# The residual of a fused Mamba and LoRA layer added by TensorE transposes in the output's PSUM bank, not by VectorE

## The reference

```python
x = x + _L0_attn_ref(_L0_cond_ref(x, itok_B_0_15, W, lora_A, lora_B), A_log, D, x_proj_w, dt_proj_w, dt_proj_b)
x = x + _L0_ffn_ref(_L0_cond2_ref(x, itok_B_6_15, base_weight, base_bias, lora_A_w, lora_B_w), router_w, A, B)

# cond:  x @ W + (x @ A[id]) @ B[id]              one adapter per batch
# attn:  dt = softplus(dt_in @ dt_proj_w.T + b)   h_t = exp(dt A) h_(t-1) + dt B_t u_t
#        y_t = sum over 16 states of h_t C_t + D u_t
# cond2: x @ W2.T + bias + LoRA of the batch
# ffn:   gates = softmax over the top 2 of 4 experts, delta = sum over experts of gate * 4 * (mid @ B.T)
```

## Time and profile before

| | |
|---|---|
| median of 3 runs | 912.07 us |
| lowest, highest | 908.38, 920.36 us |
| span of the profiled execution | 918.8 us, mean granted TensorE clock 0.958 |
| PE, DVE, ACT, POOL busy | 90%, 83%, 70%, 72% of the span |
| chain that ended last | PE 64%, DVE 9%, POOL 7%, DMA 6%, ACT 6%, issue 5% |
| from `out` 0's addition in one group to the next group's, groups 1 to 6 | 104.6, 104.2, 107.1, 109.2, 104.0 us |

### The profile page before, as it was taken

How to read it: one execution, slowest core, us unless ns; L and a number is a source line. 1 busy time by engine, 2 the same in 40 slices (tenths; PEclk the granted TensorE clock), 3 DMA queues, 4 the chain that set the end, 5 groups by cost and what they waited for, 6 DMA issues and landing times.

```text
span 918.8 us, 18601 instructions
## 1 busy us (share of the span) xinstructions
PE 830.7 (90%) x6416; PEld 769.3 (84%) x6416; DVE 764.1 (83%) x688; ACT 638.7 (70%) x1481; POOL 661.9 (72%) x344
## 2 busy tenths in 40 slices
PE   5898999899999999799997998999998999888885
PEld 4888998799888988799877997789987998677772
DVE  2437788898999799988997896998998989999993
ACT  4547678687777777777675874777776876778750
POOL 1005778688777787788876885778876887889891
PEclk9997999899999999999999998999998999889997
DMA  9978688475657557476556655576573754253221
GB/s 245 372 310 273 200 257 224 137 228 176 205 151 258 173 173 236 156 234 180 186 175 204 215 156 163 148 249 189 177 242 110 244 169 143 70 173 99 86 64 46
DMA packets 103113, 172.24 MB, mean 187 GB/s; under 512 B 21865, under 2 KB 71657, under 8 KB 94830
## 3 DMA queue, kind: packets, MB, share of 16 engines
q1 hardware_dynamic: 85614, 94.12, 34.6%
q10 hardware_dynamic: 17408, 76.95, 24.3%
HBM read 137.33 MB, written 33.69 MB: 186 GB/s over the span
## 4 chain that ended last, share of the span: by engine, by line
PE 64%; DVE 9%; POOL 7%; DMA 6%; ACT 6%; issue 5%; SPq 2%; ACTq 0%; POOLq 0%; DVEq 0%
PE jb L1043 28%; PE yp L1210 18%; PE dBx L1043 9%; POOL hC L576 7%; DVE h L1007 5%; PE yp L1043 3%; DMA dtx_scratch<-HL 3%; PE jb L1047 3%; ACT dA L610 2%; PE yp L1047 2%; DMA stacked<-dtx_scratch 1%; DMA x<-in_x 1%; DMA GA<-in_L_cond_lora_B_w 1%; PE yp L1215 1%; DVE Bd L824 1%
## 5 line engine op out<-in xcount | busy, mean ns | idle before, releaser
L576 POOL TENSOR_TENSOR hC<-h,Cb 128x1024 f32<-128x1024 f32 (+1 forms) x256 | 614.6, 2403 | 174.5 <-DVE h L1007 167.1
L1007 DVE TENSOR_TENSOR_SCAN h<-dA,dBx 128x1024 f32<-128x1024 f32 x256 | 582.7, 2280 | 57.1 <-PE dBx L1043 48.8
L610 ACT ACTIVATE dA<-dt,negA 128x252 f32<-128x252 f32 x1024 | 430.1, 494 | 64.8 <-DVE h L1007 54.5
L1210 PE MATMUL yp<-ident,hC 128*128 128x128 f32 x2048 | 280.0, 282 | 27.1 <-DVE xT L905 11.3
L1210 PEld LDWEIGHTS yp<-ident,hC 128*128 128x128 f32 x2048 | 241.0, 146 | 32.0 <-issue 27.0
L1043 PE MATMUL jb<-xT,Wst 128*128 128x256 f32 x1416 | 216.3, 296 | 0.0
L1043 PE MATMUL dBx<-Bd,stacked 96*128 96x256 f32 x1024 | 188.3, 307 | 12.0 <-DMA stacked<-dtx_scratch 6.0
L1043 PEld LDWEIGHTS jb<-xT,Wst 128*128 128x128 f32 x1416 | 184.0, 193 | 4.1 <-issue 3.3
L1043 PEld LDWEIGHTS dBx<-Bd,stacked 96*128 96x128 f32 x1024 | 147.1, 197 | 21.1 <-issue 18.9
L556 POOL TENSOR_TENSOR dtx<-dt,u 128x256 f32<-128x256 f32 x64 | 47.3, 740 | 46.4 <-DVE dt L809 43.3
L635 ACT ACTIVATE HL<-yp 128x256 fp32r<-128x256 f32 x54 | 20.4, 377 | 52.0 <-PE yp L1047 48.1
(11 more groups left out here) (165 smaller groups left out, 711.5 us busy)
## 6 DMA issues: line engine op xcount, KB each, us to landing
Wst<-W_scratch ACTq DMA_DIRECT2D x54, 1024.0 KB, 6.0
stacked<-dtx_scratch SPq DMA_DIRECT2D x192, 128.0 KB, 2.7
dtx_scratch<-HL SPq DMA_DIRECT2D x64, 256.0 KB, 3.9
Cb<-c_scratch SPq DMA_DIRECT2D x32, 512.0 KB, 5.5
xres<-in_x SPq DMA_DIRECT2D x64, 128.0 KB, 4.3
out<-obuf SPq DMA_DIRECT2D x32, 256.0 KB, 3.3
xin<-in_x ACTq DMA_DIRECT2D x26, 256.0 KB, 4.5
GB<-in_L_cond_lora_B SPq DMA_DIRECT2D x64, 64.0 KB, 5.6
```

What stands on the lines that cost most here:

```text
L576: pool.tensor_tensor(*(x[:, :, ns, :] for x in times_C(un)), ALU.mult).then_inc(hC_made, 1)
L610: act.activation(dA[:, half % NDA, :].rearrange("p (b n t) -> p b n t", b=GB_, n=HS)[:, :, n, 1:STEPS], dt[:, j % NDT, :].rearrange("p (b ...
L1007: dve.tensor_tensor_scan(h[:, un % NH, :], dA[:, half % NDA, UNIT * p:UNIT * (p + 1)], dBx[un % 2][:, :], 0.0, ALU.mult, ALU.add).then_inc ...
L1210: last = pe.matmul(y, hC[:, un % NHC, P * n:P * (n + 1)], ident[:, :], is_transpose=True, start=un == 0 and n == 0, stop=False, skip_group ...
```

## The change

The addition of x1 leaves VectorE. Ahead of the two products of an `out` job TensorE now transposes four 128x128 blocks of `x1T` back into the same bank. The first of them starts the bank's accumulation, and the two products add to it. ScalarE then copies the bank to `obuf` (the name `out` was in `LATE_ON_ACT` already, with nothing to do). It takes over the wait for the store that read the buffer before. Because the `out` jobs of group 6 now read `x1T` in group 7, the first `x1T` job of group 7 moves from unit (4, 1) to (5, 0). VectorE's initial increments of the store semaphores go, and the counts that wait for them are one store lower.

```diff
-for _at, _q in (((4, 1), job("x1T", 0, "A", ahead=0)), ((4, 3), job("A2T", 0, "A", ahead=0)), ((5, 1), job("FB", 0, "A", ahead=0)),
+for _at, _q in (((5, 0), job("x1T", 0, "A", ahead=0)), ((4, 3), job("A2T", 0, "A", ahead=0)), ((5, 1), job("FB", 0, "A", ahead=0)),
...
-                sp_e.wait_ge(s, 16 * (2 * GROUPS + 1))
+                sp_e.wait_ge(s, 16 * (2 * GROUPS))
...
 (ScalarE)
-                if name in ("xr", "mid", "rank", "gate", "out"):
+                if name in ("xr", "mid", "rank", "gate"):
                     return
...
+                elif name == "out":
+                    wait(act, out_done[i % 2], 16 * (2 * g + i // 2))
+                    act.activation(obuf[:, i % 2, :], psum[:, :], ACT.Copy).then_inc(taken[name], 1)
...
             job("gm", 0, GROUPS - 1, jb[1])
+            for i in range(4):
+                job("out", i, GROUPS - 1, jb[i % 2])
...
 (VectorE)
-                elif name == "out":
-                    dve.wait_ge(full[name], 4 * g + i + 1)
-                    dve.wait_ge(out_done[i % 2], 16 * (2 * g + i // 2 + 1))
-                    half, tt = i // 2, i % 2
-                    dve.tensor_tensor(obuf[:, i % 2, :], psum[:, :], x1[:, gpar, tt, half * 512:(half + 1) * 512], ALU.add)\
-                        .then_inc(taken[name], 1)
...
-            for s in out_done:
-                dve.sem_inc(s, 16)
...
-            for i in range(4):
-                job("out", i, G, G % 2, jb[i % 2])
...
 (TensorE)
-                    mm(psum[:, :], gm[:, 0, P * tt:P * (tt + 1)], expBT[:, of], True, False)
-                    last = mm(psum[:, :], gm[0:EM, 1, P * tt:P * (tt + 1)], expBT[0:EM, of], False, True)
+                    for a in range(K // 2):
+                        pe.matmul(psum[:, P * a:P * (a + 1)], x1T[:, K // 2 * half + a, P * tt:P * (tt + 1)], ident[:, :],
+                                  is_transpose=True, start=a == 0, stop=False, skip_group_check=True)
+                    mm(psum[:, :], gm[:, 0, P * tt:P * (tt + 1)], expBT[:, of], False, False, skip_group_check=True)
+                    last = mm(psum[:, :], gm[0:EM, 1, P * tt:P * (tt + 1)], expBT[0:EM, of], False, True, skip_group_check=True)
```

## The result

| | before | changed |
|---|---|---|
| first measurement, median | 916.22 us (4 runs, with the three shown) | 930.89 us (4 runs, 927.68 to 934.00) |
| ratio | | 1.0198, 95% interval 1.0152 to 1.0243 |
| measured again, median | 916.02 us (29 runs, 905.11 to 924.09) | 925.08 us (6 runs, 923.00 to 930.82) |
| ratio | | 1.014, 95% interval 1.0081 to 1.0198 |
| span of the profiled execution | 918.8 us | 927.1 us |

The kernel became slower. By the medians it is 14.7 us in the first measurement and 9.1 in the second; by the ratios it is about 18 and 13 us. Some executions are in a slower state of the chip; the ratios leave them out and the medians don't, and so a ratio is not the quotient of the medians beside it (1.016 and 1.010). The two intervals overlap from 1.0152 to 1.0198. The forecast's ratio was 925.3 / 912.07 = 1.0145, just under the first interval and inside the second.

What follows compares the result with a forecast made beforehand. TensorE was taken to bound most `out` jobs, ScalarE `out` 3 of groups 1 to 5. 7.5 (TensorE, body) + 2.5 (ScalarE) + 3.2 (end) = 13.2 us, from the 912.07 median to 925.3 us; range 914 to 935.

Steps and rivals of the forecast that it cites:

- The bound: At most `out` jobs of the body the chain runs through TensorE; relieving VectorE of 31 additions there gains nothing.
- The price of a transpose: On TensorE at each `out`: 0.11 us from start to start, four cost 0.44 us; 17 body jobs give 7.5 us.
- A price of 275 ns each: A full duration, 0.28 us, charged for every added transpose at the `out` jobs: 943 us; chance 0.01.
- ScalarE: At `out` 3 of groups 1 to 5 its copy delays `xT` by 0.49 us, 2.5 in all; its other copies cost zero.
- The body's sum: Groups 1 to 6: 7.5 us by TensorE at 17 `out` jobs plus 2.5 by ScalarE at five `out` 3.
- The forecast's sign: In a group without a late transfer, the window should grow from 104.5 to about 106.3 us.
- The end: Last four `out` jobs, at half clock: sixteen transposes cost 3.3 us, the copy is 0.09 shorter than the addition; sum 3.2.
- Group 7: Zero cost for the `out` jobs there, as GpSimd holds the chain; four more would cost 1.8 us if that failed.
- Series of TensorE and ScalarE: At body `out` jobs TensorE waits for ScalarE's copy, 1.07 us each at 22 jobs: 939 us; chance 0.17.
- Absorbed: DMA round trips of `stacked` shorten as they start later, the body's 10 us vanishes: 915 us; chance 0.16.
- VectorE as the bound: Freed of 31 x 0.6 = 19 us in the `out` additions, VectorE hides TensorE's part: 896 us; chance 0.02.
- The clock in the body: Added transposes let the clock fall about each `out`, doubling TensorE's 2.6 us there: 965 us; chance 0.02.

Runs made afterwards that it cites:

- the kernel with eight: The changed kernel with the four transposes of every `out` issued twice, so x1 enters twice; 935.95 us, ratio 1.017.
- TensorE's part: The changed kernel's four transposes per `out` and moved x1T job added to before, VectorE copying the bank to `obuf` instead of adding; 928.36 us, ratio 1.012.
- the body alone: The changed kernel with the last group's four `out` jobs as before, so the change is in groups 0 to 6 only; 924.48 us, ratio 1.009.
- ScalarE's part alone: The changed kernel without the transposes and with x1T where it was before, x1 missing from the output; 917.19 us, ratio 1.0026.

## Why the prediction was right

**The bound.** Right. The chain named TensorE at the `out` jobs, and what was added there came out in full, while 18.9 us taken from VectorE gave nothing (the forecast had about 21).

**The price of a transpose.** Right: 0.44 us for four on the chain, and 0.43 for four more in the kernel with eight. A price of 275 ns each would have made `out` 0 to `out` 3 grow by 12 x 0.275 = 3.3 us; it grew by 1.19. `out` 3's own is hidden, as forecast, even when doubled: 8.48 us to the wait for `xT` with and without the four in TensorE's part, 8.82 with four and with eight under ScalarE's copy.

**ScalarE.** The place was right and the size somewhat large: 0.34 us on TensorE and 0.36 or 0.37 on ScalarE at each of five `out` 3, not 0.49. At all other `out` jobs its copies cost nothing that a trace shows.

**The body's sum.** I had 1.81 us for a clean group and 10.0 in all. Measured is 1.7; five groups and group 6's four `out` (from 20.28 to 21.54 us, thus 1.3, and 0.4 behind) make 10.2. The growth has to be read from the shortest distances. The forecast's sign, a window growing from 104.5 to 106.3 us, took a window that holds waits; the clean group of before is 102.62 us by the table and that of the changed kernel 104.32. The kernel with the body alone gave 1.009, that is 8 us with 5 to 11 in its interval.

**The end.** 3.2 predicted for half clock. At half clock the four `out` took 3.0 more on TensorE in one trace, where the forecast had 3.3 less 0.09 for the copy. In the first profiled execution the clock rose on the way, and it cost 0.85 only. I had kept half clock because 5.84 us of unbroken products did not end it; both outcomes occur.

**Group 7.** I put zero there, under GpSimd's cover. The traces with before's body give 48.1, 48.1, 49.4 and 50.1 us, ScalarE's part alone 50.5; those with the transposes 48.6, 49.7, 51.4, 51.4 and 51.6. The means differ by 1.3 us and the sets overlap. The length goes with the time at half clock, which differs between kernels whose body is the same. Where two kernels have about the same amount of it, the one with transposes is at most 1 us longer (13.0 us at half clock: 50.5 without and 51.4 with; about 3 us: 48.1 and 48.6; about 7 to 8 us: 50.1 and 49.7). So the zero may be short by up to 1 us, and no run shows that the change brings more half clock: the stretches came at other places in each trace, also without the transposes. Why the first measurement's median was 930.89, and its ratio above the forecast's, stays open. Its four runs had mean granted clocks of 0.957 to 0.959, and the 29 runs of before 0.951 to 0.967.

**Where the profiled 8.3 us went.** This is less than the sum because single executions differ in late transfers and half clock. Before's group 4 lost 6.5 us between `out` 1 and 2, to a late transfer and the half clock behind it (28.09 us from `out` 0 to `out` 3 instead of 21.54); the changed one's did not. The changed one's groups 1 and 7 each had a stretch of 10.2 us at half clock. That chance is of the size of the effect. The forecast also set before's span of 918.8 against the median time and found 6.7 us; every other execution's span is 1.7 to 1.8 us under its time (927.1 of 928.93), so that before's profiled execution lay about 8.5 us above the median. So times of single executions would have shown little, and it took the distances in clean groups.

**The rivals.** Series of TensorE and ScalarE: refuted, 0.34 to 0.5 us for ScalarE's part in a group, where four copies in series needed 4 x 0.63 = 2.5, and no wait of TensorE for `obuf` in the changed kernel. The forecast's working of this rival does not hold together, though. It says that over two thirds of the `out` must be in series to pass 18.2 us, and puts half of them at 932 us, which is already past 912.07 + 18.2 = 930.3. From its own sums, 13.2 us with none and 26.7 with all in series, a bit over a third is enough. So this rival's share in the chance of slower was set on a wrong mark. Absorbed: refuted, the 1.7 us stays in the shortest groups. VectorE as the bound: refuted by the scan that waits 0.77 us once it is freed. The clock in the body: refuted. With eight transposes for each `out`, a group's granted clock was still 0.98. The Trainium skill (page "TensorE: Matmul & The Clock Gate", section "Part 4: PE-mode transpose") says of a transpose that "it doesn't count as PE-busy the same way". The 0.98 doesn't refute that, as products stand between the transposes everywhere in the body; it shows only that transposes in this share did not let the clock fall. No run here shows what transposes alone would do.

## What to carry to other kernels

Before work is moved from one engine to another, ask which of the two the chain runs through at that very place. Here 0.44 us was laid on the engine that bounds, to relieve one that waited for it 0.2 us later. Price an instruction of TensorE by the distance between starts in a row of its like, not by its duration; here they were 0.11 and 0.28 us. And where single runs scatter by more than the effect, compare the shortest instance of a repeated stage: with ten traces it resolved about 0.15 us of 103, where some 40 timed runs (12 beside 29 of before) resolved 4 to 5 us of 916.

## What the runs showed of the hardware that was not expected

- The clock at the end, after the same wait of 1.41 us for `gm`: it rose within 4 us of unbroken work in one execution (work from 916.99, full clock from about 920.7), and stayed at half for 8.8 us of it in another of the same kernel (909.54 to 918.37).
- Sixteen transposes at full clock (894.60 to 896.57), with waits of 0.87 and 1.32 us behind them, did not keep the clock up for the products: it fell about 0.5 us after these began at 899.13.
- In ten traces of nearly the same kernel, group 7 and the end were at half clock for very different times: from `out` 0's products to the end's `gm` between 2.1 and 13.5 us of about 50.
- Four transposes in a row take 0.36 to 0.44 us from start to start at full clock and 0.74 to 0.77 at half; two 128x512 products of `out` take 0.84 and 1.43.
